# Reordering the gate/up matmuls, the silu and the down projection in a fused macaron block

## The chip, the cores and the metric

The kernel runs on one NeuronCore of a Trainium2 chip. The metric is the device time of one execution, in microseconds (us). Engines are named as the profile names them: PE (TensorE) does the matmuls, PEld is its weight load, DVE (VectorE), ACT (ScalarE) and POOL (GpSimd) do elementwise work, SP issues DMAs.

## The reference, cut to what matters

An input `x` of 2 x 2048 tokens by 256 features goes through a half-step feed-forward network, a complex-valued attention, and the same feed-forward network again. The feed-forward network quantises both the activations and the weights to FP4 in blocks of 16:

```python
def fp4_quant_dequant(x):
    xb = x.reshape(shape[:-1] + (shape[-1] // BLOCK, BLOCK))
    scale = jnp.maximum(jnp.max(jnp.abs(xb), axis=-1, keepdims=True) / 6.0, 1e-12)
    idx = jnp.searchsorted(_MID, jnp.abs(xb / scale))
    return (_GRID[idx] * jnp.sign(xb / scale) * scale).reshape(shape)
gate = fp4_linear(x, w_gate)          # 256 -> 704
y = fp4_linear(x, w_up)               # 256 -> 704
h = jax.nn.silu(gate) * y
return fp4_linear(h, w_down)          # 704 -> 256
x = x + 0.5 * ffn(layernorm(x)); x = x + attention(layernorm(x)); x = x + 0.5 * ffn(layernorm(x))
```

## The kernel before, in words

The tokens are 32 tiles of 128 (`NT`). Every product is made of "high" parts and "low" remainders (the float32 value split in two fp32r numbers), so that a product takes three matmuls: high by high, high by low, low by high.

Each engine has its own instruction queue, whose order is written out by hand; semaphores join them. Nothing is planned by a scheduler: an instruction that waits holds everything behind it on its engine. In both feed-forward networks (f = 0 and f = 1) each engine runs a function `step(c, par)` for c = -2, -1, 0, ... Chain c of a step carries two things at once: the hidden values of tile c (704 wide, on their way to the down projection) and the normalised input of tile c + 4 (256 wide, on its way to gate/up). They share one row of 960 columns, `z`, and its quantisation:

- DVE (`blocks_of`, `product`): block maxima `amax` (L676), the small `s_up`, `s_neg`, `s_inv` (L679 to L688), then for the chain before it `rounded` (L698) and `grid` (L704), in the second network also the low part of the first four transposed tiles (`lower_first`, L748), then `y` = z times `s_inv` (L717), in the first network a few statistics of input tiles (L589 to L601, in two of four steps), and last `product` (L665): `z` = up columns of `gu` times `silu`.
- ACT: `absolute` (L1134), `down_out` (L1141), in the first network a mean (L1081), `chain_upper` (L1152: the transposed values, rounded, into `T_hi`), `chain_rest` (L1159 into `T_lo`, L1161), the variance (L1094), `silu_gate` (L1169), `normalise` (L1179: the input of tile c + 7 into `z`, which the next `amax` waits for), and for c = 14 to 29 of the first network `keys_normalised` (L1115).
- POOL: `residual` (L468), `scaled_x` (L475), `quantised` (L491: `zq`, which the transposes read).
- PE (`ffn_step` from L1548): `transpose_chain` (L1530, by way of L1413), eight transposes into the banks `bank2`; the first 512 of 1408 columns of gate/up for tile c + 3; `chain_lower` (L1539: two matmuls in the first network, one in the second, which subtract `T_hi` in PSUM so that the remainder stands there; it waits for ACT's `chain_upper`); the other 896 columns of gate/up; then `project_down` (17 matmuls, L1518). Gate/up is six matmuls for each of three column blocks: 512, 512 and 384.

`gu` is one buffer in PSUM (banks 0 to 2). Its gate half is columns 0 to 703, so the gate is whole when the first two blocks are; the silu reads it, and `product` reads the up half. `gu_done` is counted at the last of the 18 matmuls, `gu_read` at the end of `product`. The gate/up of tile c + 3 waits for `gu_read` of tile c + 2. After the last gated step (c = 28) `last_two` handles the chains 30 and 31.

Of the kernel before, what the change touches and what calls it, by code (L numbers as in the profile page):

```python
# [30 lines left out]
def macaron_kernel(nc, x_in, wq, bq, wk, bk, wv, bv, wo, bo, w_gate, w_up, w_down, out):  # L31
# [30 lines left out]
    with ctx:  # L62
# [6 lines left out]
        def sem(name):  # L69
            return ctx.enter_context(nc.semaphore(name))  # L70
# [122 lines left out]
        total_done, nmean_done, stats_done = sem("total_done"), sem("nmean_done"), sem("stats_done")  # L193
        var_eps, rstd_done, nmr_done = sem("var_eps"), sem("rstd_done"), sem("nmr_done")
        gu_done, silu_done, gu_read, xn_done = sem("gu_done"), sem("silu_done"), sem("gu_read"), sem("xn_done")
        amax_done, up_done, inv_done = sem("amax_done"), sem("up_done"), sem("inv_done")
        y_done, yx_done, abs_done = sem("y_done"), sem("yx_done"), sem("abs_done")
        rnd_done, grid_done, zq_done = sem("rnd_done"), sem("grid_done"), sem("zq_done")
# [39 lines left out]
        def chain(k):  # L238

            return between(k, -LEAD, NT - 1)  # L240
# [343 lines left out]
        def _(dve):  # L584
# [76 lines left out]
            def ffn_step(f):  # L661
                def product(t):

                    dve.wait_ge(silu_done, NT * f + t + 1)
                    nc.vector.tensor_tensor(out=z[:, 0:I], in0=gu[:, I:G], in1=silu[:],  # L665
                                            op=ALU.mult).then_inc(gu_read, 1)

# [325 lines left out]
        def _(act):  # L993
# [130 lines left out]
            def ffn_step(f):  # L1124
# [38 lines left out]

                def silu_gate(t):

                    act.wait_ge(gu_done, NT * f + t + 1)
                    if f or between(t, 1, NT - 1):
                        act.wait_ge(gu_read, NT * f + t)
                    nc.scalar.activation(silu[:], gu[:, 0:I], ACT.Silu).then_inc(silu_done, 1)  # L1169
# [12 lines left out]
                def step(c, par):  # L1182
                    measured = f == 0 and 0 <= c - 2 < NT - 2
                    extra = f == 0
                    if chain(c + 1):
                        absolute(c + 1)
                    if late(c) and chain(c):
                        chain_upper(c, par)
                    if extra and c == NT - 1:
                        keys_upper(0, 0)  # L1190
                    if hidden(c - 1) and c < NT:
                        down_out(c - 1, 1 - par)
                    if measured:
                        act.wait_ge(x_new, c - 1)
                        mean_of(c - 2, c - 2)
                    if c < 0:
                        silu_gate(c + 3)
                    if extra and c == 0:
                        upper_group(G1 + 2)
                    if chain(c) and not late(c):  # L1200
                        chain_upper(c, par)
                    if extra and c == -1:
                        upper_group(G1)
                    if extra and c == 0:
                        lower_group(G1 + 2)
                    if measured:
                        minus_mean(c - 2, c - 2)
                    if chain(c) and not late(c):
                        chain_rest(c, par)
                    if extra and c == -2:  # L1210
                        nv_upper()
                    if extra and c == -1:
                        upper_group(G1 + 1)
                        lower_group(G1)
                        lower_group(G1 + 1)
                    if measured:
                        variance_of(c - 2, c - 2)
                    if f and c == 2:
                        new_statistics(NQ - 1)
                    if c >= 0 and hidden(c + 3):  # L1220
                        silu_gate(c + 3)
                    if c + 7 < NT:
                        normalise(c + 7)
                    if extra and c == -2:
                        nv_lower()
                    if extra and 14 <= c < 14 + NS:
                        keys_normalised(c - 14)
                    if extra and c == NT - 1:
                        nc.scalar.activation(warm[:], mhalf[:, 0:1], ACT.Exp)
                        bias_rows()  # L1230
# [176 lines left out]
        def _(pe):  # L1407
# [93 lines left out]

            pe.wait_ge(neg_set, 1)

            def gate_up(par, columns):
                for lo, hi in columns:
                    terms = [(T, kd, w) for kd in range(KD)
                             for T, w in ((T_hi, w1_hi), (T_hi, w1_lo), (T_lo, w1_hi))]
                    for n, (T, kd, w) in enumerate(terms):
                        last = nc.tensor.matmul(gu[:, lo:hi], lhsT=T[:, par, HK + kd, :], rhs=w[:, kd, lo:hi],  # L1509
                                                start=n == 0, stop=n == len(terms) - 1)  # L1510
                return last

            def project_down(par, dn):

                terms = [(T_hi, k if k < HK else HK + KD, k, half) for k in range(HK + 1) for half in (0, D)]
                terms += [(T_lo, k, k, 0) for k in range(HK)]
                for n, (T, k, wk, half) in enumerate(terms):
                    last = nc.tensor.matmul(dn, lhsT=T[:, par, k, :], rhs=wd_hl[:, wk, half:half + D],  # L1518
                                            start=n == 0, stop=n == len(terms) - 1)
                last.then_inc(dn_done, 1)  # L1520

            def transpose_chain(f, c):
# [25 lines left out]
            def ffn_step(f):  # L1548
                def step(c, par):
                    gated = c + 3 < NT  # L1550
                    extra = f == 0
                    pe.wait_ge(lo_done, number_lo(f, c) - 1)
                    if f and hidden(c - 1):
                        pe.wait_ge(first_lo, c)
                    if extra and c == -1:
                        value_output_lower()
                    if gated and c < 0:
                        pe.wait_ge(gu_read, NT * f + c + 3)
                        gate_up(1 - par, ((0, 512), (512, 1024), (1024, G))).then_inc(gu_done, 1)
                    if extra and c == 0:  # L1560
                        transpose_group(G1 + 2)
                        pe.wait_ge(wc["lo"], G1 + 2)
                    if f and c == 0:
                        pe.wait_ge(x_att, NT)
                    transpose_chain(f, c)
                    if extra and c == -2:
                        value_output_product(0)
                    if extra and c == -1:
                        transpose_group(G1)
                    if extra and c == 0:  # L1570
                        weight_lower(G1 + 2)
                    if gated and c >= 0:
                        pe.wait_ge(gu_read, NT * f + c + 3)
                        gate_up(1 - par, ((0, 512),))
                    if extra and c == NT - 3:
                        pe.wait_ge(gu_read, NT)
                        key_bias_row()
                    chain_lower(f, c, par)
                    if extra and c == -2:
                        value_output_product(1)  # L1580
                    if extra and c == -1:
                        transpose_group(G1 + 1)
                        weight_lower(G1)
                        weight_lower(G1 + 1)
                    if gated and c >= 0:
                        gate_up(1 - par, ((512, 1024), (1024, G))).then_inc(gu_done, 1)
                    if hidden(c):
                        pe.wait_ge(lo_done, number_lo(f, c))
                        if f:
                            pe.wait_ge(first_lo, c + 1)  # L1590
                        if f or c:
                            pe.wait_ge(down_done, (NT - 1) * f + c)
                        else:
                            pe.wait_ge(wc["lo"], len(groups))
                        project_down(par, dn)

                def last_two():

# [5 lines left out]
                        value_bias_row()  # L1604
                    pe.wait_ge(late_lo, 2 * f + 1)
                    pe.wait_ge(down_done, (NT - 1) * f + NT - 2)
                    project_down(0, dn)
                    pe.wait_ge(late_lo, 2 * f + 2)
                    project_down(1, dn_last)
                    if f == 0:  # L1610
                        transpose_keys(0, 1)

# [37 lines left out]
            pe.wait_ge(wc["lo"], G1)  # L1650
            pe.wait_ge(aw["m_lo"], 1)
            pe.wait_ge(lo_done, number_lo(0, -4))
            gate_up(0, ((0, 512), (512, 1024), (1024, G))).then_inc(gu_done, 1)
            transpose_chain(0, -3)
            transpose_wo(0)
            query_bias()
# [191 lines left out]
            chain_lower(1, -4, 0)  # L1848
            weighted_values(n, 1)
            pe.wait_ge(lo_done, number_lo(1, -4))  # L1850
            gate_up(0, ((0, 512), (512, 1024), (1024, G))).then_inc(gu_done, 1)
            transpose_chain(1, -3)
            weighted_values(n, 2)
            chain_lower(1, -3, 1)
# [31 lines left out]
```

## Time and profile before

| What | Value |
|---|---|
| median of 3 runs | 985.06 us (982.87 to 985.18) |
| profiled execution | 983.04 us, span 981.3 us |
| PE busy | 930.5 us, 95% of the span |
| DVE, ACT, POOL busy | 709.9 us (72%), 655.1 us (67%), 505.4 us (52%) |
| chain that ended last | PE 67%, DVE 15%, POOL 6%, ACT 6%, issue 4% |
| gate/up matmuls (L1509) | 3 x 384, 437 us busy, overlapping each other |
| down matmuls (L1518) | 1088 |
| granted TensorE clock | mean 0.991 of full |

A busy time is the sum in which an engine had an instruction running. PE's matmuls overlap at their ends, so what one costs is read from the distance between starts. The chain that ended last is followed backwards from the last instruction through whatever released each step.

### The profile page before, as it was taken

The page shows a single profiled execution, that of the slowest core. Times are in us where ns is not written, and L with a number is a line of the kernel's source. Part 1 is how long each engine was busy: PE and PEld are TensorE (multiplying, and loading weights), DVE is VectorE, ACT ScalarE, POOL GpSimd, SP SyncE. Part 2 cuts the span into 40 slices and gives each one's busy share as a digit, 9 for nine tenths or more (in the row PEclk, how much of TensorE's full clock was granted, in tenths as well). Part 3 has the DMA queues.
Part 4 walks back from the last instruction along what each step waited for, and adds up shares of the span by engine and source line. Part 5 has one row for each costly group of instructions (what it writes and reads, how often), then busy time and mean ns, then how long its engine had stood idle before and what let it go on. Part 6 is the DMA issues. An engine that isn't in the chain of part 4 may idle for free.

```text
span 981.3 us, 18219 instructions
## 1 busy us (share of the span) xinstructions
PE 930.5 (95%) x6607; PEld 867.3 (88%) x6607; DVE 709.9 (72%) x1180; ACT 655.1 (67%) x1380; POOL 505.4 (52%) x593
## 2 busy tenths in 40 slices
PE   3889999999989999999999999999988999999997
PEld 2778888888879899999999999999987888888886
DVE  7889888888757755565555555555567889998996
ACT  5767778888775776666666666666673655556553
POOL 3445576666530455554545355555562556566552
PEclk9899999999999999999999999999989999999999
DMA  9000000000000000000000000000000000000001
GB/s 321 30 1 1 1 1 2 1 1 1 1 1 1 2 2 1 1 1 1 1 1 1 2 1 1 2 1 2 1 1 1 1 23 22 22 22 23 22 1 43
DMA packets 11560, 13.94 MB, mean 14 GB/s; under 512 B 848, under 2 KB 10576, under 8 KB 11472
## 3 DMA queue, kind: packets, MB, share of 16 engines
q1 hardware_dynamic: 11472, 12.79, 3.9%
q8 instruction: 53, 0.87, 0.4%
q14 instruction: 35, 0.29, 0.1%
HBM read 8.59 MB, written 4.19 MB: 13 GB/s over the span
## 4 chain that ended last, share of the span: by engine, by line
PE 67%; DVE 15%; POOL 6%; ACT 6%; issue 4%; DMA 1%; SPq 0%; DVEq 0%; ACTq 0%
PE bank L1725 18%; PE bank L1509 15%; POOL zq L491 6%; PE bank L1413 5%; PE bank_b L1518 3%; DVE amax L676 3%; DVE rounded L698 3%; DVE grid L704 3%; PE bank_b L1777 3%; PE bank_b L1773 3%; PE bank L1773 3%; PE bank L1777 3%; PE bank L1775 3%; PE bank_b L1775 3%; DVE z L665 2%
## 5 line engine op out<-in xcount | busy, mean ns | idle before, releaser
L529 POOL TENSOR_TENSOR p_lo<-s_buf,p_hi 128x512 fp32r<-128x512 f32 x128 | 164.9, 1293 | 210.0 <-ACT p_hi L1316 203.4
L491 POOL TENSOR_TENSOR zq<-grid,s_neg 128x64 f32<-128x64 f32 (+2 forms) x188 | 177.8, 971 | 62.4 <-DVE grid L704 52.2
L1509 PE MATMUL bank<-w_hi,T_hi 128*128 128x512 f32 (+1 forms) x384 | 149.3, 389 | 0.9 <-ACT T_lo L1159 0.8
L1725 PE MATMUL bank<-q_hi,k_hi 128*128 128x256 f32 x512 | 145.2, 284 | 0.1
L1725 PE MATMUL bank<-q_lo,k_hi 128*128 128x256 f32 x512 | 144.9, 283 | 0.0
L1725 PE MATMUL bank<-q_hi,k_lo 128*128 128x256 f32 x512 | 144.8, 283 | 0.0
L1509 PE MATMUL bank<-w_hi,T_lo 128*128 128x512 f32 (+1 forms) x384 | 144.2, 376 | 0.0
L1509 PE MATMUL bank<-w_lo,T_hi 128*128 128x512 f32 (+1 forms) x384 | 143.8, 374 | 0.0
L1301 ACT ACTIVATE s_buf<-bank 128x512 f32<-128x512 f32 x128 | 76.4, 597 | 95.8 <-PE bank L1725 95.8
L857 DVE TENSOR_TENSOR top<-bank,top 128x512 f32<-128x512 f32 x96 | 66.4, 692 | 66.8 <-ACT s_buf L1301 66.8
L1169 ACT ACTIVATE silu<-bank 128x704 f32<-128x704 f32 x64 | 48.6, 760 | 81.4 <-PE bank L1509 81.4
L1518 PE MATMUL bank_b<-wd_hl,T_hi 128*128 128x256 f32 x744 | 99.0, 281 | 3.5 <-ACT T_hi L1161 2.9
L1518 PEld LDWEIGHTS bank_b<-wd_hl,T_hi 128*128 128x128 f32 x744 | 94.9, 189 | 5.8 <-ACT T_hi L1161 3.6
L1725 PEld LDWEIGHTS bank<-q_hi,k_hi 128*128 128x128 f32 x512 | 98.1, 192 | 0.3 <-issue 0.2
L1725 PEld LDWEIGHTS bank<-q_hi,k_lo 128*128 128x128 f32 x512 | 98.2, 192 | 0.0
L1725 PEld LDWEIGHTS bank<-q_lo,k_hi 128*128 128x128 f32 x512 | 98.2, 192 | 0.0
L665 DVE TENSOR_TENSOR z<-bank,silu 128x704 f32<-128x704 f32 x64 | 56.9, 890 | 50.1 <-ACT silu L1169 49.9
L475 POOL TENSOR_TENSOR y<-z,s_inv 128x256 f32<-128x256 f32 x56 | 35.3, 631 | 108.1 <-DVE rounded L698 108.1
L1152 ACT ACTIVATE T_hi<-bank 128x1024 fp32r<-128x1024 f32 (+1 forms) x72 | 68.7, 954 | 31.1 <-PE bank L1413 30.3
L1307 ACT ACTIVATE s_buf<-s_buf 128x512 f32<-128x512 f32 x128 | 77.0, 629 | 18.2 <-DVE s_buf L879 18.2
L1413 PE MATMUL bank<-ident,zq 128*128 128x128 f32 x528 | 71.6, 277 | 13.5 <-POOL zq L491 8.6
L879 DVE TENSOR_TENSOR s_buf<-s_buf,bank 128x512 f32<-128x512 f32 x128 | 78.6, 680 | 7.7 <-PE bank L1413 7.5
(202 smaller groups left out, 2540.1 us busy)
## 6 DMA issues: line engine op xcount, KB each, us to landing
out<-x SPq DMA_DIRECT2D x7, 512.0 KB, 2.9
x<-in_L_attn_hidden_states SPq DMA_DIRECT2D x3, 1024.0 KB, 14.0
x<-in_L_attn_hidden_states SPq DMA_DIRECT2D x2, 512.0 KB, 8.3
wraw<-in_L_ffn_w_down SPq DMA_DIRECT2D x1, 704.0 KB, 9.4
wraw<-in_L_ffn_w_gate SPq DMA_DIRECT2D x1, 640.0 KB, 4.4
wraw<-in_L_ffn_w_up SPq DMA_DIRECT2D x1, 640.0 KB, 7.0
wq_s<-in_L_attn_Wq SPq DMA_DIRECT2D x1, 512.0 KB, 8.2
wk_s<-in_L_attn_Wk SPq DMA_DIRECT2D x1, 512.0 KB, 10.0
```

What stands on the lines that cost most here:

```text
L491: last = nc.gpsimd.tensor_tensor(out=blocks(zq[:, to:to + hi - lo]), in0=blocks(grid[:, lo:hi]), in1=spread(s_neg[:, par, lo // BLOCK:hi / ...
L529: nc.gpsimd.tensor_tensor(out=p_lo[:, n % 2, 2 * c:2 * c + 2, :], in0=score_buf(n, c), in1=p_hi[:, 2 * c:2 * c + 2, :].bitcast(F32), op=AL ...
L665: nc.vector.tensor_tensor(out=z[:, 0:I], in0=gu[:, I:G], in1=silu[:], op=ALU.mult).then_inc(gu_read, 1)
L857: nc.vector.tensor_tensor(out=top[:], in0=score_bank(c), in1=other, op=ALU.max).then_inc(top_done, 1)
L879: nc.vector.tensor_tensor(out=p, in0=p, in1=shift_bank.unsqueeze(1).to_broadcast([P, 2, QT * P]), op=ALU.subtract).then_inc(diff_done, 1)
L1152: nc.scalar.activation(T_hi[:, par, t, :], bank[:, t, :], ACT.Copy).then_inc(hi_done, 1)
L1301: nc.scalar.activation(score_buf(n, c), score_bank(c), ACT.Copy).then_inc(evac_done, 1)
L1307: nc.scalar.activation(p, p, ACT.Exp, scale=SCALE).then_inc(exp_done, 1)
L1413: return nc.tensor.matmul(dst, lhsT=src, rhs=ident[:], is_transpose=True, start=first, stop=True, skip_group_check=True)
L1509: last = nc.tensor.matmul(gu[:, lo:hi], lhsT=T[:, par, HK + kd, :], rhs=w[:, kd, lo:hi], start=n == 0, stop=n == len(terms) - 1)
L1518: last = nc.tensor.matmul(dn, lhsT=T[:, par, k, :], rhs=wd_hl[:, wk, half:half + D], start=n == 0, stop=n == len(terms) - 1)
L1725: last = nc.tensor.matmul(score_bank(c)[:, a, :], lhsT=kk[:, kd, t], rhs=q[:, n % 2, kd, :], start=i == 0 and a == 0, stop=i == len(terms) ...
```

## The change

PE: in a gated step the first 512 columns of gate/up now stand ahead of the tile's transposes, at the start of the step; the second block stands between the transposes and `chain_lower`; the third after `chain_lower`. Steps with c < 0 keep their order. The wait for `gu_read` moves with the first block to the start of the step; the wait for the second network's `first_lo` moves behind that block. A new semaphore `gate_done` is counted after the second block. ACT: the silu waits for `gate_done` instead of `gu_done`, and for c >= 0 it stands between `chain_upper` and `chain_rest` instead of behind the variance. DVE: `product` waits for both the silu and `gu_done`. The down projection is split: ten high products first, then the waits for `lo_done` and `first_lo`, then the two high products of the last 64 hidden rows and the five low ones. No arithmetic instruction is added or removed.

```diff
@@ product (DVE) @@
                     dve.wait_ge(silu_done, NT * f + t + 1)
+                    dve.wait_ge(gu_done, NT * f + t + 1)
@@ silu_gate (ACT) @@
-                    act.wait_ge(gu_done, NT * f + t + 1)
+                    act.wait_ge(gate_done, NT * f + t + 1)
@@ step (ACT) @@
                         minus_mean(c - 2, c - 2)
+                    if c >= 0 and hidden(c + 3):
+                        silu_gate(c + 3)
                     if chain(c) and not late(c):
                         chain_rest(c, par)
...
-                    if c >= 0 and hidden(c + 3):
-                        silu_gate(c + 3)
                     if c + 7 < NT:
                         normalise(c + 7)
@@ PE @@
+            def gate_up(par, part):
+                lo, hi = ((0, 512), (512, 1024), (1024, G))[part]
...
+                if part == 1:
+                    last.then_inc(gate_done, 1)
+                if part == 2:
+                    last.then_inc(gu_done, 1)
+            def project_down_first(par, dn):
+                terms = [(k, half) for k in range(HK) for half in (0, D)]
...
+            def project_down_rest(par, dn):
+                terms = [(T_hi, HK + KD, HK, half) for half in (0, D)] + [(T_lo, k, k, 0) for k in range(HK)]
...
@@ step (PE) @@
                     pe.wait_ge(lo_done, number_lo(f, c) - 1)
-                    if f and hidden(c - 1):
-                        pe.wait_ge(first_lo, c)
+                    if gated:
+                        pe.wait_ge(gu_read, NT * f + c + 3)
+                        gate_up(1 - par, 0)
                     if gated and c < 0:
-                        pe.wait_ge(gu_read, NT * f + c + 3)
-                        gate_up(1 - par, ((0, 512), (512, 1024), (1024, G))).then_inc(gu_done, 1)
+                        gate_up(1 - par, 1)
+                        gate_up(1 - par, 2)
...
+                    if f and hidden(c - 1):
+                        pe.wait_ge(first_lo, c)
                     transpose_chain(f, c)
                     if gated and c >= 0:
-                        pe.wait_ge(gu_read, NT * f + c + 3)
-                        gate_up(1 - par, ((0, 512),))
+                        gate_up(1 - par, 1)
                     chain_lower(f, c, par)
                     if gated and c >= 0:
-                        gate_up(1 - par, ((512, 1024), (1024, G))).then_inc(gu_done, 1)
+                        gate_up(1 - par, 2)
                     if hidden(c):
-                        pe.wait_ge(lo_done, number_lo(f, c))
-                        if f:
-                            pe.wait_ge(first_lo, c + 1)
                         ...
-                        project_down(par, dn)
+                        project_down_first(par, dn)
+                        pe.wait_ge(lo_done, number_lo(f, c))
+                        if f:
+                            pe.wait_ge(first_lo, c + 1)
+                        project_down_rest(par, dn)
```

## Rows read from the trace of the kernel before

**Rows 1.** Windows; us, then busy PE, PEld, DVE, ACT, POOL (count), clock, DMA, GB/s.
```profile
200.00:250.00 50.00, 49.08 (x296) 43.06 (x297) 43.33 (x63) 41.44 (x95) 29.25 (x38) 1.00 0.00 1
...
850.00:900.00 50.00, 49.39 (x309) 43.77 (x308) 45.41 (x64) 29.25 (x49) 29.62 (x36) 1.00 0.04 12
```
**Rows 2.** Timeline: silu of tiles 3 and 31, both networks; start, us, instruction, idle before.
```profile
64.86 0.76 ACT L1169 ACTIVATE silu<-bank 128x704 f32<-128x704 f32 x1 [1.22 <-PE bank L1509]
...
272.36 0.76 ACT L1169 ACTIVATE silu<-bank 128x704 f32<-128x704 f32 x1 [0.59 <-PE bank L1509]
...
759.21 0.76 ACT L1169 ACTIVATE silu<-bank 128x704 f32<-128x704 f32 x1 [1.65 <-PE bank L1509]
...
961.01 0.76 ACT L1169 ACTIVATE silu<-bank 128x704 f32<-128x704 f32 x1 [1.65 <-PE bank L1509]
```
**Rows 3.** Chain of waits, second network, near its end; start, us.
```profile
949.15 0.87 PE bank L1413 x8
950.02 1.38 PE bank L1509 x6
951.40 0.24 PE bank L1539
...
954.06 2.00 PE bank_b L1518 x17
```
**Rows 4.** Timeline of PE, first network, one round.
```profile
101.44 1.58 PE L1518 MATMUL bank_b<-wd_hl,T_hi 128*128 128x256 f32 x12
...
103.44 1.04 PE L1413 MATMUL bank<-ident,zq 128*128 128x128 f32 x8
...
105.71 0.62 PE L1539 MATMUL bank<-T_hi,neg_ident 128*128 128x512 f32 x2
...
108.60 1.10 PE L1518 MATMUL bank_b<-wd_hl,T_hi 128*128 128x256 f32 x8
```
**Rows 5.** Waits from 60 to 280, then 780 to 950; us in total, times, longest.
```profile
DVE z L665 <- ACT silu L1169: 26.0, 21, 2.1
...
DVE z L665 <- ACT silu L1169: 11.6, 22, 1.0
...
PE bank L1413 <- POOL zq L491: 1.7, 10, 0.2
```
**Rows 6.** Timeline of ACT, one round of the first network's later part.
```profile
228.05 0.76 ACT L1169 ACTIVATE silu<-bank 128x704 f32<-128x704 f32 x1 [0.59 <-PE bank L1509]
228.70 0.59 ACT L1179 ACTIVATE z<-x,nmr,rstd 128x256 f32<-128x256 f32 x1
...
231.29 1.03 ACT L1152 ACTIVATE T_hi<-bank 128x1024 fp32r<-128x1024 f32 x1
...
233.14 0.92 ACT L1159 ACTIVATE T_lo<-bank 128x896 fp32r<-128x896 f32 x1 [0.65 <-PE bank L1539]
```
**Rows 7.** Timeline of DVE, the same round.
```profile
229.91 1.15 DVE L676 TENSOR_REDUCE amax<-z 128x60 f32<-128x960 f32 x1
231.09 0.74 DVE L679 SCALAR_TENSOR_TENSOR s_up<-amax,c_up 128x60 f32<-128x60 f32 x1
...
234.53 0.88 DVE L717 TENSOR_TENSOR y<-z,s_inv 128x704 f32<-128x704 f32 x1
```
**Rows 8.** Groups by line, 60 to 280: input statistics; busy us, mean ns, idle before.
```profile
L589 DVE BATCH_NORM_STATS2 stats<-x 128x6 f32<-128x256 f32 x20 | 7.5, 418 | 0.3
```
**Rows 9.** Timeline of ACT, second network, step 2.
```profile
771.61 0.27 ACT L1161 ACTIVATE T_hi<-bank 64x128 fp32r<-64x128 f32 x1
...
774.91 0.76 ACT L1169 ACTIVATE silu<-bank 128x704 f32<-128x704 f32 x1
```
**Rows 10.** Timeline, second network: the `zq` of a middle step.
```profile
867.30 2.88 POOL L491 TENSOR_TENSOR zq<-grid,s_neg 128x256 f32<-128x256 f32 x3 [0.50 <-DVE grid L704]
```
**Rows 11.** Timeline of the second network's end.
```profile
960.00 1.70 DVE L717 TENSOR_TENSOR y<-z,s_inv 128x704 f32<-128x704 f32 x1
...
967.09 2.18 PE L1518 MATMUL bank_b<-wd_hl,T_hi 128*128 128x256 f32 x12 [1.63 <-ACT T_hi L1161]
```

More of the change, by code:

```diff
@@ L195, in macaron_kernel @@
         gu_done, silu_done, gu_read, xn_done = sem("gu_done"), sem("silu_done"), sem("gu_read"), sem("xn_done")
+        gate_done = sem("gate_done")
         amax_done, up_done, inv_done = sem("amax_done"), sem("up_done"), sem("inv_done")
@@ L1502, in _ @@
             pe.wait_ge(neg_set, 1)
[L1504 to L1516, printed above, removed]
+            def gate_up(par, part):
+                lo, hi = ((0, 512), (512, 1024), (1024, G))[part]
+                terms = [(T, kd, w) for kd in range(KD)
+                         for T, w in ((T_hi, w1_hi), (T_hi, w1_lo), (T_lo, w1_hi))]
+                for n, (T, kd, w) in enumerate(terms):
+                    last = nc.tensor.matmul(gu[:, lo:hi], lhsT=T[:, par, HK + kd, :], rhs=w[:, kd, lo:hi],
+                                            start=n == 0, stop=n == len(terms) - 1)
+                if part == 1:
[4 more added lines that the diff above has]
+                terms = [(k, half) for k in range(HK) for half in (0, D)]
+                for n, (k, half) in enumerate(terms):
+                    nc.tensor.matmul(dn, lhsT=T_hi[:, par, k, :], rhs=wd_hl[:, k, half:half + D],
+                                     start=n == 0, stop=False)
+            def project_down_rest(par, dn):
+                terms = [(T_hi, HK + KD, HK, half) for half in (0, D)] + [(T_lo, k, k, 0) for k in range(HK)]
                 for n, (T, k, wk, half) in enumerate(terms):
                     last = nc.tensor.matmul(dn, lhsT=T[:, par, k, :], rhs=wd_hl[:, wk, half:half + D],
-                                            start=n == 0, stop=n == len(terms) - 1)
+                                            start=False, stop=n == len(terms) - 1)
                 last.then_inc(dn_done, 1)
@@ L1606, in last_two @@
                     pe.wait_ge(down_done, (NT - 1) * f + NT - 2)
-                    project_down(0, dn)
+                    project_down_first(0, dn)
+                    project_down_rest(0, dn)
                     pe.wait_ge(late_lo, 2 * f + 2)
-                    project_down(1, dn_last)
+                    project_down_first(1, dn_last)
+                    project_down_rest(1, dn_last)
                     if f == 0:
@@ L1652, in _ @@
             pe.wait_ge(lo_done, number_lo(0, -4))
-            gate_up(0, ((0, 512), (512, 1024), (1024, G))).then_inc(gu_done, 1)
+            for columns in range(3):
+                gate_up(0, columns)
             transpose_chain(0, -3)
@@ L1850, in _ @@
             pe.wait_ge(lo_done, number_lo(1, -4))
-            gate_up(0, ((0, 512), (512, 1024), (1024, G))).then_inc(gu_done, 1)
+            for columns in range(3):
+                gate_up(0, columns)
             transpose_chain(1, -3)
```

## The prediction, made before the changed kernel ran

> **What bounds the kernel now.** I read the page's busy times, then the same times in windows of 50 us, then single rounds of the timeline, then the waits of each network. PE is busy 49.1 and 49.4 of 50 us in the middles of the two networks, DVE 43.3 and 45.4 [rows 1]: PE is nearly full, DVE close behind, so a new order can win only PE's small stalls. How large these are is read by setting the mean round against a round that PE alone fills. Between the silus of tiles 3 and 31 lie 28 rounds: (272.36 - 64.86)/28 = 7.41 us in the first network, (961.01 - 759.21)/28 = 7.21 us in the second [rows 2]. Near the end of the second network the chain of waits runs through PE alone: transposes at 949.15, down projection at 954.06 for 2.00 us, next transposes at 956.06, a round of 6.91 us [rows 3]. In the first network the down projections at 101.44 and 108.60 give 7.16 us [rows 4] (one 512-column matmul more in `chain_lower`). So PE loses at most 28 x 0.25 = 7.0 us in the first and 28 x 0.30 = 8.3 us in the second network, and the attention between them is not touched.
>
> What holds PE is a loop over three steps: transposes, gate/up, silu, product, quantisation, transposes. DVE waits for the silu 26.0 us in the first network's 220 us and 11.6 us in the second's 170 us [rows 5], some 0.9 and 0.5 us a round, and at its other end the transposes wait for `zq` (1.7 us shown [rows 5]; the weight load before them hides the rest). In the first network's later rounds ACT is the late one: silu at 228.05, and only at 231.29, straight behind other work, `chain_upper` [rows 6], which `chain_lower` needs.
>
> **The change, part by part.** I count from the start of `chain_lower`, t = 0. A 512-column block takes 1.38 us, the down projection 2.00 [rows 3].
>
> *Order on PE.* The same 45 or 44 matmuls a step, so PE's floor stays 7.16 and 6.91. `gu_done` used to come 2.89 us behind `chain_lower` (108.60 - 105.71 [rows 4]), 2.66 in the second network [rows 3]; with one block fewer behind it, 1.51 and 1.28. Against the transposes it comes 1.4 us earlier, and `zq` gets 1.4 us more time: the transposes of the next step start at 1.51 + 2.00 + 1.38 = 4.9 us (second network 4.7). Their `zq` takes 2.88 us on POOL [rows 10] from a grid that ends near 0: 1.7 us of slack where there was none.
>
> *Silu ahead of `chain_rest`.* The gate is whole at about t = 0.2, the silu runs 0.2 to 0.9, while the subtraction of `chain_lower` runs; it cost DVE about 0.9 us on the loop and now costs nothing there. `chain_rest` starts at 0.9 instead of 0.7 (first network; 0.4 in the second) and is over at 0.9 + 0.92 + 0.27, about 2.1 [rows 6]. Queued behind the silu are `chain_rest`, variance, `normalise`, `absolute`. Waiting for `lo_done` is the second part of down, at 1.51 + 10/17 x 2.00 = 2.7: the split down projection hides the silu; without the split it would cost 0.6 us a round. For ACT's lateness: `down_out` and the mean now have the first block as well as the transposes to run beside, 1.4 us against the 0.3 by which they were late, so that stall goes.
>
> *The product waits for `gu_done`.* It starts at about 1.5 + 0.2 = 1.7, ends 2.65. The first block, now at the head of the step, needs it at 3.5 (second network 3.3): 0.8 us of slack, against 1.2 before. If it is late, everything of the step on PE is late, the transposes too.
>
> *`normalise` is later.* In the first network it now stands behind `chain_rest` and the variance and ends at about 2.1 + 0.5 + 0.6 = 3.2; `amax` needs it, and could start at 2.7. DVE from `amax` to the end of `y` took 234.53 + 0.88 - 229.91 = 5.5 us with `s_up` at 0.74 [rows 7], 5.0 when `s_up` is short. So the product is ready at 3.2 + 5.0 to 5.5 - 7.16 = 1.0 to 1.5, no loss in plain rounds. Two of four rounds (c up to 21) hold input statistics: two at 0.42 us [rows 8] in one, and those with four aggregates and two small operations, about 1.95, in the next. There it comes at 3.0 to 3.5, ends 0.95 later and holds PE by 0.5 to 1.0 us. Five such rounds: 3.5 us. The second network has no variance there: `normalise` ends near 2.3, `amax` starts at 2.45, no wait. DVE's own round is 7.21 - 0.5 = 6.7 us (its mean less its wait [rows 2, 5]), under 6.91.
>
> *Step 2 of the second network.* ACT has 3.0 us of statistics between 771.61 + 0.27 and 774.91 [rows 9], which held the silu; now they hold `normalise` and thus `amax`. I keep 1.5 us of loss there, and 0.6 us for semaphore jitter in all other rounds.
>
> *Ends.* At the last product DVE alone leads to the end: it starts 0.7 to 0.8 us earlier. In step 29 the down projection waited 1.63 us for `chain_rest` (967.09 [rows 11]); ten of its matmuls now run beside it, and the next transposes, which followed it, come up to 0.4 us sooner on the chain. 1.1 us for each network. The ramps (c < 0) get the silu one block early: 0.5 us together, between 0 and 3.
>
> *The shared port.* `y` takes 0.88 us when it runs free [rows 7] and 1.70 when it starts 0.4 us behind a 704-wide `zq` of POOL [rows 11]. In the second network `lower_first` now waits for `T_hi` at t = -0.1, so `y` may slip 0.1 to 0.3 us into POOL's wide piece. One slip of 0.8 us makes the product end at 3.2 to 3.3, just within its slack, and DVE catches up at 0.2 us a round. I take zero, bounds 0 and 0.8 us a round. The Trainium skill, page "SBUF — State Buffer", section "SBUF: two separate sides", says that VectorE operations with two SBUF inputs and GpSimd operations that read SBUF hold their common port exclusively, the second fully blocked; the two durations of `y` agree with it, and by it the change is at the mercy of a few tenths of a microsecond in the start of `y` (third rival).
>
> *Sum.* First network 28 x 0.25 - 3.5 = 3.5; second 28 x 0.30 - 1.5 - 0.6 = 6.2; ends 2.2; ramps 0.5: 12.4 us. From the profiled execution, 983.04: 970.6. It lies 2.0 us under the median of the runs, from which it would be 972.7; I say 972.0.
>
> **Rivals.** *Half of it.* DVE's loop, with later `normalise` and statistics, holds the first network at 7.41; the second gives its 6.2 and the ends 1: 985 - 7 = 978. For: DVE at 43 of 50 us with uneven rounds. Against: its wait of 0.9 us a round.
>
> *Nothing.* The rounds are set by DVE and POOL already, and PE's waits only change their name: 984. Against: in the rounds at 6.91 and 7.16 all other engines kept up.
>
> *Slower.* `y` is blocked in each round of both networks (+0.8) and `s_up` stands at 0.74 in the first. With the deadline of the product at 2.4, the first network's round is 3.2 + 5.5 + 0.8 + 0.7 (statistics on average) - 2.4 = 7.8 plus 0.1 for jitter, against 7.41: +14 us; the second's 6.6 + 0.8 = 7.4 against 7.21: +5; less 3 of ends and ramps: 1001. It decides where DVE's round passes about 7.4; for it speaks one row of 1.70 us, against it that a late DVE leaves the collision again and that PE, not DVE, then has the longer wait before it.
>
> **How the numbers follow.** Forecast 0.72; half 0.12; nothing 0.09; slower 0.07. A difference under 0.3% (3 us) can't be told from none. Faster is then 0.84, same 0.09, slower 0.07. Lower end: all stalls go (15.3), ends 2.2, ramps 2: 985 - 19.5 = 965.5. Upper end: the half case with some of its own loss, 981. That leaves out the cases nothing and slower, and little of the forecast.
>
> **What would show it.** In the trace after: rounds between silus of tiles 3 and 31 of 7.2 to 7.35 us (first) and 6.9 to 7.0 (second); DVE no longer waiting for the silu but a few tenths for `gu_done` or `T_hi`; no wait of PE for `zq` in the middle; `amax` waiting for `normalise` in the first network, 0.3 to 0.6 us a round; a stall of 0.5 to 1 us at the first block in the rounds with statistics; `chain_lower` in the first network right behind its block. The forecast is wrong if the second network's round stays above 7.1, if `y` is at 1.7 in most rounds, or if PE waits at the second part of down.

## The result and the profile after

The changed kernel takes 973.08 us (median of 4 runs, 971.3 to 974.74), the kernel before 983.96 in the runs beside it (4 runs, 982.11 to 985.18): a ratio of 0.9891, 95% interval 0.9869 to 0.9914, 10.9 us faster. 972.0 was predicted. The profiled execution took 971.3 us with a span of 969.5, 11.8 us under that of before.

The same two windows as in [rows 1], of the kernel after (us, busy PE, PEld, DVE, ACT, POOL with counts, clock, DMA, GB/s):

```profile
200.00:250.00 50.00, 49.77 (x314) 44.64 (x313) 42.84 (x65) 42.89 (x98) 32.35 (x42) 1.00 0.00 1
850.00:900.00 50.00, 50.00 (x317) 44.88 (x317) 48.52 (x66) 31.23 (x51) 30.25 (x36) 1.00 0.07 22
```

PE has no idle time left in the second network (50.00 against 49.39), and DVE has gone from 45.4 to 48.5 of 50 us. The silus of tiles 3 and 31, as in [rows 2], from the timeline of ACT:

```profile
62.60 0.76 ACT L1171 ACTIVATE silu<-bank 128x704 f32<-128x704 f32 x1 [0.20 <-PE bank L1512]
...
265.23 0.76 ACT L1171 ACTIVATE silu<-bank 128x704 f32<-128x704 f32 x1 [0.17 <-PE bank L1512]
...
751.51 0.76 ACT L1171 ACTIVATE silu<-bank 128x704 f32<-128x704 f32 x1 [0.37 <-PE bank L1512]
...
947.99 0.76 ACT L1171 ACTIVATE silu<-bank 128x704 f32<-128x704 f32 x1 [0.35 <-PE bank L1512]
```

28 rounds take 202.6 us, 7.24 each, in the first network (before 7.41) and 196.5 us, 7.02 each, in the second (7.21): 4.9 and 5.3 of the 11.8 us. The other 1.6 us are a sum of opposite signs. The silu has moved within PE's step, so I count the rest from the start of the down projection, ahead of which PE does the same work in both orders. To the last residual of the network it then takes 20.66 us at the end of the first (before 19.03) and 17.81 at the end of the second (17.82). The start of the kernel is 0.75 us shorter (63.91 against 64.66) and the stretch between the networks 2.4 us (465.4 against 467.8). These last two are not a property of the change: in a second profile of the same kernel (*changed, again* below) they take 65.5 and 466.9 us, together 0.1 us less than before, while its rounds take 202.6 and 196.5 again.

One round of the second network, in the chain of waits of the kernel after, against [rows 3]: all of it is PE, in the new order, with the down projection in two parts.

```profile
937.40 1.39 PE bank L1512 x6
938.79 0.87 PE bank L1415 x8
939.66 1.38 PE bank L1512 x6
941.04 0.23 PE bank L1551
941.27 1.04 PE bank L1512 x6
942.31 1.18 PE bank_b L1523 x10
943.49 0.82 PE bank_b L1530 x7
944.31 1.39 PE bank L1512 x6
```

944.31 - 937.40 = 6.91 us, the floor that was read from before, and the distance of nearly all silus from tile 10 on. The waits from 60 to 280 us, against the first of [rows 5] (us in total, times, longest):

```profile
DVE z L667 <- PE bank L1512: 17.4, 18, 2.2
DVE amax L678 <- ACT z L1181: 9.2, 18, 0.5
...
PE bank L1512 <- DVE z L667: 1.1, 5, 0.2
```

The product waits for the up columns, no longer for the silu, and by about 1 us each time where a few tenths were forecast. `amax` waits 0.5 us a round for `normalise`, a new wait that was expected. PE waits for the product in five rounds: every fourth distance between silus up to the twentieth is 7.62 to 7.64 us, all others 7.14 to 7.16. One of these rounds in the timeline:

```profile
171.08 0.63 PE L1551 MATMUL bank<-T_hi,neg_ident 128*128 128x512 f32 x2
...
172.15 0.75 DVE L590 BATCH_NORM_STATS2 stats<-x 128x6 f32<-128x256 f32 x2
...
173.66 0.59 ACT L1181 ACTIVATE z<-x,nmr,rstd 128x256 f32<-128x256 f32 x1
...
173.96 0.88 DVE L667 TENSOR_TENSOR z<-bank,silu 128x704 f32<-128x704 f32 x1
...
174.99 0.47 PE L1512 MATMUL bank<-w_hi,T_hi 128*128 128x512 f32 x1 [0.24 <-DVE z L667]
```

The statistics stand between `y` and the product, which starts 2.9 us behind `chain_lower` instead of 1.8, and the first block 3.9 instead of 3.5. In the second network, step 2 loses 1.7 us (8.58 against 6.91), where `amax` waits 2.16 us for `normalise` behind ACT's new statistics, and step 0 loses 1.1 us (7.98).

### The profile page after: what moved, and what is told of

Read it like the earlier page. It is cut to its first block, busy times and chain, and to the rows that moved or that the text cites. A ratio compares the mean times of both kernels' runs of the same rounds, so it can differ in the third digit from the quotient of the medians.

```text
span 969.5 us, 18233 instructions
## 1 busy us (share of the span) xinstructions
PE 923.2 (95%) x6607; PEld 865.2 (89%) x6607; DVE 708.0 (73%) x1180; ACT 656.7 (68%) x1380; POOL 505.6 (52%) x593
## 4 chain that ended last, share of the span: by engine, by line
PE 80%; DVE 11%; ACT 5%; issue 3%; POOL 1%; DMA 0%; SPq 0%; DVEq 0%; ACTq 0%
PE bank L1512 21%; PE bank L1743 18%; PE bank L1415 7%; PE bank_b L1523 6%; PE bank_b L1530 4%; PE bank_b L1795 3%; PE bank L1791 3%; PE bank_b L1791 3%; PE bank_b L1793 3%; PE bank L1793 3%; PE bank L1795 3%; PE bank L1698 2%; PE bank L1551 2%; DVE grid L706 1%; DVE amax L678 1%
## 5 line engine op out<-in xcount | busy, mean ns | idle before, releaser
L678 DVE TENSOR_REDUCE amax<-z 128x60 f32<-128x960 f32 (+2 forms) x72 | 75.0, 1041 | 21.5 <-ACT z L1181 17.6
L1512 PEld LDWEIGHTS bank<-w_hi,T_hi 128*128 128x128 f32 x384 | 72.5, 189 | 13.9 <-issue 5.2
L1523 PE MATMUL bank_b<-wd_hl,T_hi 128*128 128x256 f32 x620 | 84.1, 281 | 0.0
L469 POOL TENSOR_TENSOR x<-x,down 128x256 f32<-128x256 f32 x62 | 46.7, 753 | 68.7 <-ACT down L1143 68.7
L1512 PEld LDWEIGHTS bank<-w_hi,T_lo 128*128 128x128 f32 x384 | 72.3, 188 | 10.8
```

Of the source, the lines that this page charges most:

```text
L678: nc.vector.tensor_reduce(out=amax[:, n], in_=blocks(z[:, lo:hi]), axis=AX_X, op=ALU.max, apply_absolute_value=True).then_inc(amax_done, 1)
L1523: nc.tensor.matmul(dn, lhsT=T_hi[:, par, k, :], rhs=wd_hl[:, k, half:half + D], start=n == 0, stop=False)
```

## The experiments

The theory: PE's work is the floor (7.15 and 6.91 us); what lies above it are waits of a loop, and the three parts of the change need one another, because each gives the others their cover or their deadline. The rivals: one part carries the gain by itself (the order, which frees the transposes from `zq`, or the early silu). The table has the mean of the 28 distances between silus in each network, in the profiled execution.

| Kernel | first network | second | median us | ratio to before, 95% interval |
|---|---|---|---|---|
| before | 7.41 | 7.21 | 982.4 to 984.0 | |
| changed | 7.24 | 7.02 | 973.08 | 0.9869 to 0.9914 |
| order alone | 8.13 | 7.24 | 1003.64 | 1.0179 to 1.0222 |
| order undone | 7.89 | 7.03 | 990.95 | 1.0051 to 1.0092 |
| down whole | 7.89 | 7.47 | 1001.85 | 1.0158 to 1.0197 |
| silu late | 8.11 | 7.12 | 999.16 | 1.0137 to 1.0170 |
| first block on silu | 7.15 | 6.96 | 966.70 | 0.9813 to 0.9851 |
| normalise first | 7.16 | 6.99 | 971.23 | 0.9838 to 0.9897 |
| both of these | 7.15 | 6.95 | 968.32 | 0.9825 to 0.9869 |
| split alone | 7.41 | 7.20 | 987.91 | 1.0032 to 1.0072 |
| step 29 whole | 7.24 | 7.02 | 972.03 | 0.9858 to 0.9902 |
| block on silu, step 29 whole | 7.15 | 6.96 | 963.35 | 0.9779 to 0.9818 |
| changed, again | 7.24 | 7.02 | 974.57 | 0.9889 to 0.9916 |
| block on silu, step 29 whole, again | 7.15 | 6.95 | 964.43 | 0.9789 to 0.9816 |

**Order alone.** From the changed kernel:

```diff
-                    act.wait_ge(gate_done, NT * f + t + 1)
+                    act.wait_ge(gu_done, NT * f + t + 1)
@@ step (ACT): silu_gate(c + 3) back behind variance_of @@
@@ step (PE) @@
-                        project_down_first(par, dn)
                         pe.wait_ge(lo_done, number_lo(f, c))
                         if f:
                             pe.wait_ge(first_lo, c + 1)
+                        project_down_first(par, dn)
                         project_down_rest(par, dn)
```

> Only the new order of the gate/up blocks on PE; the silu waits for the whole gate/up and stands behind the variance again, the down projection is whole. My theory: the order moves the deadline of the product from 5.7 to 3.5 us behind chain_lower, and in the first network the silu, behind chain_rest and variance (ends near 2.4), lets the product end near 4.05: PE waits 0.5 to 0.6 us at the first block in each of 28 rounds, first network 7.7 us a round. Second network, without a variance: product ends near 3.2, no wait, 6.9 to 7.0. Total 984 to 988, no gain. Rival (the order alone frees the transposes from zq and carries the gain): first network at most 7.25, total 973 to 976.

1003.64 us. The direction was the theory's, and the rival is out, but the loss in the first network is twice the one expected: 8.13 us a round, not 7.7. The middle of the second network runs at 7.09, where 6.9 to 7.0 was expected.

**Silu late.** The changed kernel with one edit on ACT:

```diff
-                    if c >= 0 and hidden(c + 3):
-                        silu_gate(c + 3)
                     if chain(c) and not late(c):
                         chain_rest(c, par)
...
+                    if c >= 0 and hidden(c + 3):
+                        silu_gate(c + 3)
                     if c + 7 < NT:
                         normalise(c + 7)
```

> The changed kernel with the silu back behind chain_rest and variance on ACT (still released by the gate columns). My theory: in the first network the silu ends near 3.05 us behind chain_lower, the product near 4.0, the first block waits 0.5 us in each round: 7.65 to 7.7 us a round; in the second network the silu ends near 1.9 and the product still makes its deadline: 6.91 to 7.0. Total 984 to 988. Rival (what counts is that the gate columns release the silu, not where it stands): first network 7.2 to 7.3, total 973 to 975.

999.16 us, where 984 to 988 was expected. The second network comes to 6.91 a round behind its first three distances (7.95, 9.93 and 8.44, which make its mean 7.12), as the theory had it for the middle; the first comes to 8.11. The timeline of this kernel shows why 0.5 us was too little:

```profile
200.70 0.63 PE L1551 MATMUL bank<-T_hi,neg_ident 128*128 128x512 f32 x2
...
203.22 0.76 ACT L1171 ACTIVATE silu<-bank 128x704 f32<-128x704 f32 x1
...
204.07 0.89 DVE L667 TENSOR_TENSOR z<-bank,silu 128x704 f32<-128x704 f32 x1 [1.63 <-ACT silu L1171]
...
205.11 0.47 PE L1512 MATMUL bank<-w_hi,T_hi 128*128 128x512 f32 x1 [0.74 <-DVE z L667]
```

The silu starts 2.52 us behind `chain_lower` (2.35 was reckoned), the product 3.37 (3.05), and the next first block 4.41: the product needs 1.04 us from its start to PE's, not 0.95. The block is thus 0.9 us late (plain rounds have it at 3.51), and the rounds are nearly 0.1 us longer than that. Small errors of one sign made 0.5 us into 1.0. Since the loss was already there in the order alone, the place of the silu is what decides in the first network, not what releases it.

**Order undone.** PE's order of before, with the early silu and the split:

```diff
@@ step (PE) @@
-                    if gated:
+                    if gated and c < 0:
                         pe.wait_ge(gu_read, NT * f + c + 3)
                         gate_up(1 - par, 0)
...
                     if gated and c >= 0:
-                        gate_up(1 - par, 1)
+                        pe.wait_ge(gu_read, NT * f + c + 3)
+                        gate_up(1 - par, 0)
                     chain_lower(f, c, par)
                     if gated and c >= 0:
+                        gate_up(1 - par, 1)
                         gate_up(1 - par, 2)
```

> The changed kernel with PE's old order (first block behind the transposes), but the silu early and the down projection split. My theory: the gate is whole only 2.05 us behind chain_lower, ACT stands at the silu until then with chain_rest, variance, normalise, absolute, down_out and the mean behind it, and comes 1 us late to chain_upper: first network near 8.0 us a round, second network 6.95 to 7.0, total near 994. Rival (the early silu is what shortens the loop, whatever the order): both networks at or below 7.2, total 975 to 979.

990.95 us (near 994 was expected); 7.75 us a round in the first network, 8.24 where ACT also has `keys_normalised`; 6.91 in the second from its eighth distance on. Its timeline in the first network:

```profile
151.96 1.01 ACT L1154 ACTIVATE T_hi<-bank 128x1024 fp32r<-128x1024 f32 x1
...
153.03 0.72 PE L1551 MATMUL bank<-T_hi,neg_ident 128*128 128x512 f32 x2 [0.35 <-ACT T_hi L1154]
...
155.17 0.76 ACT L1171 ACTIVATE silu<-bank 128x704 f32<-128x704 f32 x1 [2.02 <-PE bank L1512]
...
158.18 1.15 DVE L678 TENSOR_REDUCE amax<-z 128x60 f32<-128x960 f32 x1 [0.98 <-ACT z L1181]
```

ACT stands 2.02 us at the silu, with the rest of its step behind it, and reaches `chain_upper` late, without any wait of its own. The theory holds for the first network. In the middle of the second network the new order is not needed: the early silu and the split take the rounds to PE's floor without it, as the new order and the split do without the early silu (*silu late*). The early silu by itself, without the split, was not run.

**Down whole.** The changed kernel without the split (the last hunk of the first experiment alone).

> The changed kernel with the waits for the remainders ahead of the whole down projection. My theory: the silu pushes chain_rest behind the third block, and all of down waits for it: 0.55 us a round in the first network (remainder ready 0.54 us behind where down starts in the trace) and 0.35 in the second: 28 x 0.9 = 25 us, less the stalls of the statistics rounds which it covers (2.4): 994 to 998. Rival (the split is there for the last steps only, the middle hides it): within 2 us of 973.

1001.85 us, 28.8 us above the changed kernel where 21 to 25 were expected. The first network loses 0.65 us a round instead of 0.55 (7.89 against 7.24), the second 0.45 instead of 0.35 (7.47 against 7.02). The timeline of the second network:

```profile
884.12 0.69 DVE L750 TENSOR_TENSOR T_lo<-bank,T_hi 128x512 fp32r<-128x512 f32 x1 [0.15 <-ACT T_hi L1154]
...
884.72 2.03 DVE L719 TENSOR_TENSOR y<-z,s_inv 128x704 f32<-128x704 f32 x1
...
885.59 0.27 ACT L1163 ACTIVATE T_hi<-bank 64x128 fp32r<-64x128 f32 x1
...
885.96 1.38 PE L1523 MATMUL bank_b<-wd_hl,T_hi 128*128 128x256 f32 x10 [0.28 <-issue]
```

Down starts 0.1 us behind ACT's L1163, so it is the split that hides the silu ahead of `chain_rest`. This row also shows the collision of the prediction's last rival: `lower_first` waits 0.15 us for `T_hi`, `y` slips behind the start of POOL's 704-wide `zq` (884.62) and takes 2.03 us instead of 0.93; 8 of the 23 `y` between 780 and 950 us are so long. By the Trainium skill, page "SBUF — State Buffer", section "SBUF: two separate sides", of a VectorE operation with two SBUF inputs and a GpSimd operation that reads SBUF the second is fully blocked until the first is over. The row agrees with that: `y` ends at 886.75, 0.74 us behind the wide `zq` (886.01). In the changed kernel the slip does not occur (20 `y` between 800 and 940 us, longest 0.94); that DVE is too busy there for it is my reading, which no run tests.

**Split alone.** The kernel before, with the split of down only.

> The kernel before with nothing but the split of the down projection (its waits for the remainders behind ten high products). My theory: in the middle the remainders are ready before down starts, so the rounds stay at 7.41 and 7.21 us; only step 29 of each network gains, at most 1.2 us each: total 982 to 984, nothing that can be told. Rival (the split by itself takes stalls away): 980 or less.

The rounds are unchanged (7.41 and 7.20), as expected, but the kernel is not the same: 987.91 us (10 runs, 983.1 to 990.9), 0.3 to 0.7% slower. The theory had a gain at the ends; there is a loss. From the last product to the last residual the second network takes 18.84 us against 16.76 before, with a granted clock of 0.50 from 973 to 978 us behind a pause of 3.02 us; the first takes 18.51 against 17.97 at a granted clock of 1.00, since DVE's last piece of `zq` runs into a moved `residual` of POOL and takes 0.75 us instead of 0.22. The mean granted clock of its ten executions is 0.984 to 0.993, that of the kernel before beside it 0.990 to 0.996.

**The deadline of the first block.** Block 0 fills one PSUM bank that only the silu reads, the product reads the other two:

```diff
                     if gated:
-                        pe.wait_ge(gu_read, NT * f + c + 3)
+                        pe.wait_ge(silu_done, NT * f + c + 3)
                         gate_up(1 - par, 0)
                     if gated and c < 0:
+                        pe.wait_ge(gu_read, NT * f + c + 3)
...
                     if gated and c >= 0:
+                        pe.wait_ge(gu_read, NT * f + c + 3)
                         gate_up(1 - par, 1)
```

> The changed kernel, but the first gate/up block (columns 0 to 511, a bank that only the silu reads) waits for the silu of the tile before, and the product's wait stands ahead of the second block. My theory: what is left of stalls in the middle is the product missing its deadline (0.47 us in five statistics rounds, 1.1 in step 0 and 1.7 in step 2 of the second network); a deadline 2.2 us later takes all of it: first network 7.15 to 7.17 a round, second 6.92 to 6.95, total 968 (967 to 969.5). Rival (the stalls only move to the transposes, which then wait for zq, or to DVE, which fills 6.8 of 6.9 us in the second network): no more than 1 us gained, 972 or more.

966.7 us (965.3 to 967.3). Every round of the first network is 7.14 to 7.16 us, step 0 of the second 7.09, and step 2 of it 7.74 instead of 8.58; the theory is right for the rounds, and the total gain, 6.4 us against the 973.08 of the changed kernel (in other executions), is a little above the 4 to 6 it gave. The side-by-side below is the better comparison.

**Normalise first.** `normalise(c + 7)` ahead of `variance_of` and `new_statistics`.

> The changed kernel with ACT's normalise ahead of the variance (first network) and of the new statistics (second network, step 2). My theory: the 0.5 us that amax waits for normalise in each round of the first network is what the statistics rounds lack, so their 0.47 us stalls go (2.4 us); step 2 of the second network keeps a stall of about 0.75 of its 1.7 us, because absolute still stands behind the statistics: total 969.5 to 970.5. Rival (the statistics on DVE alone make the rounds late): the stalls stay at 0.4 us or more, total 972 to 973.

971.23 us, between 965.4 and 973.0: too wide for the total to tell: the executions at a mean granted clock of 0.993 take 965.4 and 965.7 us, those at 0.986 take 972.4 to 973.0. The profile does: the statistics rounds fall from 7.63 to 7.20 to 7.24 us, step 2 of the second network from 8.58 to 7.71, step 0 stays at 7.98. So it was the wait for `normalise`, not the statistics alone, that made those rounds late.

**Both.**

> Both of the two edits together. My theory: they remove the same stalls of the first network, so that they do not add: 967.5 to 968.5, within 0.5 us of the first alone. Rival (two separate losses): 965 or less.

968.32 us (965.4 to 969.9), 1.6 us above the first edit alone beside it, with rounds of 7.15 and 6.95 us: the same stalls are removed, they do not add. The higher total lies outside the rounds: its profile reaches tile 3's silu at 62.49 us against 60.95, takes 1.2 us more between the networks, and its executions have mean clocks of 0.986 to 0.991 against 0.989 to 0.991. At 0.989 the two take 966.6 and 966.7 to 967.3 us, at 0.991 they take 965.4 and 965.3 to 965.7.

**The ends.** Step 29 has no gate/up to stand beside the down projection:

```diff
-                        project_down_first(par, dn)
+                        if gated:
+                            project_down_first(par, dn)
                         pe.wait_ge(lo_done, number_lo(f, c))
                         if f:
                             pe.wait_ge(first_lo, c + 1)
+                        if not gated:
+                            project_down_first(par, dn)
                         project_down_rest(par, dn)
```

> The changed kernel, but in step 29 of each network (which has no gate/up) the down projection waits for its remainders as a whole again. My theory: the split there ends PE's work early, leaves it idle for 3.0 to 3.1 us ahead of the transposes of tile 31, and the granted clock falls to half for what follows; with 17 matmuls later by 1.2 us the gap is near 2 us and the clock holds: from the last product to the end 18.6 to 19.4 us instead of 20.1, and from the last product of the first network to its last residual 18 to 19 instead of 20.4; total 970 to 971. Rival (the longer end comes from DVE, whose absolute value waits on ACT): the ends stay, total 972 to 974.

972.03 us (969.5 to 972.6), a gain that the total can't tell from none. In the trace it is there at the end of the first network and absent at the end of the second (17.49 us from last product to last residual, 17.51 without the edit). The first network's end in the changed kernel, the transposes of tile 31 and the windows around them (clock after the five engines):

```profile
278.10 1.97 PE L1415 MATMUL bank<-ident,zq 128*128 128x128 f32 x8 [3.08 <-DVE zq L771]
```
```profile
275.00:278.00 3.00, 0.02 (x1) 0.00 (x0) 2.93 (x5) 2.59 (x8) 0.93 (x3) 0.92 0.00 0
278.00:281.00 3.00, 2.90 (x14) 2.91 (x15) 1.07 (x3) 0.90 (x1) 0.00 (x0) 0.52 0.00 0
```

and the same with step 29's down projection whole:

```profile
278.49 1.09 PE L1415 MATMUL bank<-ident,zq 128*128 128x128 f32 x8 [1.57 <-DVE zq L771]
```
```profile
275.00:278.00 3.00, 1.92 (x17) 1.68 (x16) 2.38 (x3) 1.47 (x3) 0.86 (x2) 1.00 0.00 0
278.00:281.00 3.00, 2.51 (x20) 2.44 (x21) 1.79 (x5) 2.93 (x9) 0.73 (x1) 1.00 0.00 0
```

With the split PE finishes early, idles 3.08 us and works on at a granted clock of 0.52, that is at 1.2 GHz; eight transposes take 1.97 us. Whole, PE idles 1.57 us and stays at 2.4 GHz; they take 1.09, and the end from the last product to the last residual, 20.36 us with the split, is 18.74; 1.4 of the 1.6 us lie behind the start of the transposes.

At the end of the second network the pause is only shortened, and the clock falls with the split and without it. Tile 31's transposes and the window from 962 to 964 us, changed kernel, then step 29 whole:

```profile
960.15 1.97 PE L1415 MATMUL bank<-ident,zq 128*128 128x128 f32 x8 [3.03 <-DVE zq L771]
962.00:964.00 2.00, 2.00 (x13) 2.00 (x13) 0.78 (x1) 1.02 (x1) 0.00 (x0) 0.61 0.00 0
```
```profile
961.08 1.62 PE L1415 MATMUL bank<-ident,zq 128*128 128x128 f32 x8 [2.48 <-DVE zq L771]
962.00:964.00 2.00, 2.00 (x12) 2.00 (x11) 0.27 (x2) 1.03 (x1) 0.00 (x0) 0.50 0.11 37
```

The transposes start 10.8 us behind the last product in both.

> The kernel whose first block waits for the silu alone, with the same edit of step 29. My theory: its ends (20.7 and 18.5 us from last product to last residual, clock at half after the gap) lose 1.5 to 2 us each: total 962 to 964.5. Rival: 966 to 967.

963.35 us (962.3 to 963.8), as the theory had it. Side by side on one chip with the changed kernel:

> The changed kernel itself, on the chip of the next run, so that the two are compared side by side: 971 to 974.5, as before.

> The best version again (first block waits for the silu; step 29 with the down projection whole), on the same chip as the changed kernel. My theory: 9 to 11 us under it: 5 from the first block's deadline, 2 to 3 from the ends, the rest from a clock that holds at the gap ahead of the second network's first transposes, which differs from run to run: 962 to 965. Rival (the clock's share was luck): 965 to 967.

974.57 us (973.0 to 974.7) and 964.43 us (963.9 to 965.2), a difference of 10.1 us between kernels run beside each other; against the kernel before the best version stands at 0.9803 (0.9789 to 0.9816). The clock at the gap ahead of the second network's transposes was indeed luck. The two profiles of this version differ there: the pause was 3.26 us in the earlier and 4.09 in the later. The window from 715 to 720 us, first in the earlier profile, then in the later one,

```profile
715.00:720.00 5.00, 5.00 (x35) 4.58 (x34) 3.58 (x8) 4.73 (x19) 3.73 (x6) 1.00 0.00 2
```
```profile
715.00:720.00 5.00, 4.97 (x24) 5.00 (x25) 2.89 (x7) 3.36 (x11) 4.02 (x6) 0.50 0.01 2
```

after which tile 3's silu of the second network comes at 744.18 and at 747.11 us; the gain over the changed kernel stood without it. Of all fourteen profiles only the earlier one has a clock of 1.00 behind this gap.

## Why the prediction was right, point by point

*The floor and the room above it.* 6.91 us a round, and 7.15 where 7.16 was read, are where the rounds settled. Setting the mean round against a stall-free one gave the right size of the possible gain before any part of the change was reasoned about.

*First network, 3.5 predicted, 4.9 measured.* The mechanism was right in its pieces: no loss in plain rounds, `amax` waiting 0.5 us for `normalise`, five late rounds at the statistics. The mis-sized term is the late round: 0.5 to 1.0 us was reckoned, I took 0.7, and it measured 0.47. *Normalise first* shows its cause to be the one that was named.

*Second network, 6.2 predicted, 5.3 measured.* Step 2 lost 1.7 us where 1.5 was kept. Step 0 lost 1.1, which the sum did not have: DVE does the last of the attention's residuals there, and the product misses a deadline that the new order had moved forward. *The deadline of the first block* takes it to 0.2.

*Ends, 2.2 predicted; -1.6 measured.* The step that failed is the 1.1 us for each network: "it starts 0.7 to 0.8 us earlier" for the product, and "ten of its matmuls now run beside it, and the next transposes, which followed it, come up to 0.4 us sooner". Both happen, and neither shortens the end of the first network. Tile 31 waits for DVE, and DVE for ACT's `absolute`, which stands behind `chain_rest` of step 29 (3.08 us of DVE's idle time before `rounded` in the changed kernel, 1.98 before). PE's finished work only lengthened its pause, and behind it the granted clock was 0.52: that end is 1.6 us longer than before. With step 29's down projection whole it is as long as before (19.03 us from the start of step 28's down projection in both). At the end of the second network the gain is used up by the clock: the pause ahead of tile 31's transposes is 3.03 us where it was 1.19, and from their start to the last residual it takes 6.72 us where it took 5.68. There undoing the split left a pause of 2.48 us, and the clock fell as well.

*Start and middle, 0.5 predicted, 3.2 measured in the profiled pair.* Most of this is luck. The second profile of the changed kernel has 0.1 us there, and the stretch between the networks alone differs by 3.0 us between two profiles of the best version.

*Silu, split, order.* That the split hides the silu was right (*down whole*: 0.65 and 0.45 us a round; the prediction had 0.6). The prediction counts the early silu as part of the gain of both networks; in the first the new order does lose without it, in the middle of the second it does not. The slower rival did not come: `y` stayed at 0.93 us in the rounds of the changed kernel, though one edit was enough to bring it to 2.03 in a third of the rounds of the second network.

Measured less predicted, the terms are +1.4 (first network), -0.9 (second), -3.8 (ends) and +2.7 us (start and middle); the sum is 0.6 us too large (12.4 against the 11.8 of the spans). So the rounds were forecast well (9.7 against 10.2 us), and that the total came out within 1.1 us of the median is cancellation: a term with the wrong sign against one that another execution of the same kernel does not show.

## What to carry to other kernels

Where one engine is full, read one stall-free round and multiply the difference to the mean: that is all that a reordering can win in these rounds. Ends and ramps have to be reckoned by themselves. An early release is worth its time only if what is pushed behind it has a cover of its own; here the new order alone lost 2.0% and the split alone 0.5%, every kernel with one of the three edits taken back was slower than the one before, by 0.7 to 1.8%, and the three together won 1.1%. When a wait moves to the head of a step, ask which part of the buffer it protects: waiting for the reader of one bank instead of the last reader of all three was worth another 0.7%, and with the end of the split repaired 1.0% side by side.

## What the runs showed of the hardware that was not expected

Finishing PE's work sooner in front of a fixed wait can cost time: at the end of the first network a pause of 3.08 us was followed by a granted clock of 0.52 over the next 3 us, one of 1.57 us by 1.00. The length of the pause alone does not decide it. In the second profile of the changed kernel the transposes behind a pause of 3.07 us still took 1.09 us; the clock was 0.50 only behind them, from 281 to 284 us. In *split alone* a pause of 2.73 us was followed by 1.00, and in the kernel before the pause of 1.63 us of [rows 11] was followed by 0.50 from 968 to 970 us:

```profile
968.00:970.00 2.00, 2.00 (x12) 2.00 (x11) 1.07 (x2) 0.76 (x1) 0.76 (x1) 0.50 0.00 0
```

Ahead of the second network's first transposes PE pauses for 4.0 to 4.1 us in nine of the fourteen profiles and for 3.3 us in five. Over the 2 us behind it the granted clock is 0.50 in twelve of them, 0.73 in *order undone* (pause 4.04 us) and 1.00 in one profile (3.26 us), whose kernel had 0.50 in its other profile (4.09 us). The stretch between the networks is 3.0 us shorter in that one profile than in the other of its kernel, 0.8 of it in the pause itself.
